# Two slots' score tiles in one visit to the 64-row mode, every second slot, and the places of the probs x values bursts

## The reference

```python
# block L0, 16 heads of 16
q = layer_norm(x, ln1) @ q_w + q_b;  k = ctx @ k_w + k_b;  v = ctx @ v_w + v_b
attn = softmax(where(mask, q @ k.T * 0.25, min))        # 256 x 512 for each head and batch
h = (attn @ v) @ cproj_w + cproj_b + x
h = h + gelu(layer_norm(h, ln2) @ fc_w + fc_b) @ proj_w + proj_b
# block L1, one head of 256, same context
out = h + alpha * (softmax((h @ w_q.T) @ (ctx @ w_k.T).T / 16) @ (ctx @ w_v.T)) @ w_o.T
```

## Time and profile before

| | us |
|---|---|
| median of 3 runs | 340.21 |
| lowest and highest | 338.55, 342.17 |
| the profiled execution | 339.22 |
| its span on the core | 337.4 |
| PE busy | 294.4 (87%) |
| DVE, ACT, POOL busy | 201.4 (60%), 177.4 (53%), 94.0 (28%) |

### The profile page before, as it was taken

How to read it: one execution, slowest core, us unless ns; L and a number is a source line. 1 busy time by engine, 2 the same in 40 slices (tenths; PEclk the granted TensorE clock), 3 DMA queues, 4 the chain that set the end, 5 groups by cost and what they waited for, 6 DMA issues and landing times.

```text
span 337.4 us, 5437 instructions
## 1 busy us (share of the span) xinstructions
PE 294.4 (87%) x2073; PEld 215.1 (64%) x2073; DVE 201.4 (60%) x372; ACT 177.4 (53%) x330; POOL 94.0 (28%) x122
## 2 busy tenths in 40 slices
PE   3996899986977799999968898999989989989895
PEld 2682656753555677656846676665846767768884
DVE  5627856547754867566455787556457464254944
ACT  1431746458453486757351596655545378625612
POOL 2552512103011158430010278420021136143200
PEclk9997559979696999999976999999999699999999
DMA  5799344425502024161130032133030000000001
GB/s 167 193 178 150 92 160 132 106 38 109 143 5 95 25 44 79 30 149 50 28 127 4 26 66 57 59 48 77 14 112 1 3 0 2 2 0 0 2 31 33
DMA packets 14478, 22.26 MB, mean 66 GB/s; under 512 B 3229, under 2 KB 7917, under 8 KB 14429
## 3 DMA queue, kind: packets, MB, share of 16 engines
q1 hardware_dynamic: 10608, 13.97, 19.4%
q0 software_dynamic: 1456, 3.87, 4.2%
q10 hardware_dynamic: 2388, 4.07, 3.8%
HBM read 10.50 MB, written 1.05 MB: 34 GB/s over the span
## 4 chain that ended last, share of the span: by engine, by line
PE 67%; DVE 14%; ACT 6%; issue 5%; POOL 3%; DMA 2%; ACTq 1%; DVEq 0%; POOLq 0%
PE work_ps L620 14%; PE work_ps L607 9%; PE s L676 8%; DVE neg_max L1427 7%; PE om L703 7%; PE work_ps L624 6%; PE s L693 5%; PE s L607 3%; PE s L620 2%; PE om L683 2%; ACT q_stack L1106 2%; PE work_ps L753 1%; POOL max_cols L1746 1%; DVE cT_l L1403 1%; DMA probs<-in_L_xattn_q_w_dram 1%
## 5 line engine op out<-in xcount | busy, mean ns | idle before, releaser
L1427 DVE TENSOR_REDUCE neg_max<-s 128x1 f32<-128x512 f32 x128 | 84.1, 685 | 77.7 <-PE s L676 77.5
L1114 ACT ACTIVATE probs<-s 128x512 f32<-128x512 f32 x128 | 75.1, 597 | 47.0 <-PE s L693 46.3
L693 PE MATMUL s<-q_stack,k_stack 57*128 57x256 f32 x256 | 63.1, 350 | 1.8 <-ACT probs L1114 1.2
L676 PE MATMUL s<-k_stack,q_stack 57*128 57x512 f32 x128 | 59.0, 523 | 3.0 <-DVE neg_max L1427 1.8
L693 PEld LDWEIGHTS s<-q_stack,k_stack 57*128 57x128 f32 x256 | 40.0, 206 | 11.6 <-issue 4.2
L676 PEld LDWEIGHTS s<-k_stack,q_stack 57*128 57x128 f32 x128 | 24.3, 214 | 23.7 <-DVE neg_max L1427 12.8
L703 PE MATMUL om<-probs,vals 128*17 128x256 f32 x512 | 36.0, 403 | 0.1
L1746 POOL CAST max_cols<-neg_max 128x8 fp32r<-128x8 f32 x16 | 5.7, 358 | 96.8 <-DVE neg_max L1427 96.8
L703 PEld LDWEIGHTS om<-probs,vals 128*17 128x17 f32 x512 | 12.2, 100 | 15.6 <-issue 5.7
L1106 ACT ACTIVATE q_stack<-om 8x1024 fp32r<-8x1024 f32 x16 | 16.1, 1008 | 10.2 <-PE om L683 10.1
L1128 ACT ACTIVATE y_h<-work_ps 128x512 fp32r<-128x512 f32 x12 | 7.2, 596 | 15.8 <-PE work_ps L624 14.8
(11 more groups left out here) (317 smaller groups left out, 698.7 us busy)
## 6 DMA issues: line engine op xcount, KB each, us to landing
k_stack<-kp_h SPq DMA_DIRECT2D x32, 128.0 KB
cx<-in_ctx_dram SPq DMA_DIRECT2D x4, 512.0 KB, 4.7
k_stack<-kp_l SPq DMA_DIRECT2D x16, 128.0 KB
q_stack<-qp_h SPq DMA_DIRECT2D x28, 64.0 KB
pcx<-in_ctx_dram ACTq DMA_DIRECT2D x3, 512.0 KB, 4.8
xz<-in_x_dram SPq DMA_DIRECT2D x4, 256.0 KB, 4.1
raw_late<-in_L_xattn_fc_w_dram POOLq DMA_DIRECT2D x1, 1024.0 KB, 5.3
raw_late<-in_L_xattn_proj_w_dram POOLq DMA_DIRECT2D x1, 1024.0 KB, 7.0
```

The source lines that it names most:

```text
L676: pe.matmul(s1[:, s1_bank(b, SLOTS * g + s), :], q_stack[half, hd, chunk(t)], k_stack[half, hd, :], start=True, stop=True).then_inc(s1_ful ...
L693: mm = pe.matmul(s2[:, s2_bank(b, SLOTS * g + s), i * LQ:(i + 1) * LQ], k_stack[half, hd, chunk(k)], q_stack[half, hd, :], start=True, sto ...
L1114: act.activation(probs[:, g % 2, s // 2, k:k + 2, :], s2[:, s2_bank(b, SLOTS * g + s), :].rearrange("p (k n) -> p k n", k=2), ACT.Exp).the ...
L1427: dve.tensor_reduce(neg_max[:, g % 2, s % 2, s // 2:s // 2 + 1], s1[:, s1_bank(b, SLOTS * g + s), :], AX.X, ALU.max, negate=True).then_inc ...
```

## The change

`attend` on PE issues score tiles in slots with even s only, for the slots s and s + 1 together. `MAX_TILES` is now keyed by the even slots, and DVE has a table of its own, `TAKE_AT`, for the slot in which each maximum is taken. Bursts 0 and 1 move from behind the visit of s = 1 to ahead of the visit of s = 0; bursts 2 and 3 from behind the visit of s = 3 to behind the visit of s = 2. The turning of the maxima stays at s = 6 and now comes behind the exp tiles of both 6 and 7. The tables of the pre and post steps and the lists of ACT, POOL and SP are unchanged.

```diff
-MAX_TILES = ((0, 1), (2, 3), (4,), (5,), (6,), (7,), (), ())
+MAX_TILES = {0: (0, 1), 2: (2, 3, 4), 4: (5, 6, 7), 6: ()}
+TAKE_AT = ((0, 1), (), (2, 3), (4,), (5, 6), (7,), (), ())
-PV_AT = {1: (0, 1), 3: (2, 3)}
+PV_BEFORE, PV_AFTER = {0: (0, 1)}, {2: (2, 3)}
@@ PE, attend @@
-                tiles = MAX_TILES[s] if nb < B else ()
-                for i in tiles[:1]:
-                    max_tile(nb, ng, i)
-                if s == 0:
-                    pe.wait_ge(rows_in, NG * b + g + 1)
-                exp_tile(b, g, s)
-                for i in tiles[1:]:
-                    max_tile(nb, ng, i)
-                if s in PV_AT and pb_ >= 0:
-                    for k in PV_AT[s]:
+                if s in PV_BEFORE and pb_ >= 0:
+                    for k in PV_BEFORE[s]:
+                        pv(pb_, pg, k)
+                if s % 2 == 0:
+                    tiles = MAX_TILES[s] if nb < B else ()
+                    for e in range(2):
+                        for i in tiles[e:e + 1]:
+                            max_tile(nb, ng, i)
+                        if s == e == 0:
+                            pe.wait_ge(rows_in, NG * b + g + 1)
+                        exp_tile(b, g, s + e)
+                    for i in tiles[2:]:
+                        max_tile(nb, ng, i)
+                if s in PV_AFTER and pb_ >= 0:
+                    for k in PV_AFTER[s]:
                         pv(pb_, pg, k)
@@ DVE, attend @@
-                    for i in MAX_TILES[s]:
+                    for i in TAKE_AT[s]:
                         take_max(nb, ng, i)
```

## The result

The changed kernel takes 365.95 us in the median of 4 runs (361.64 to 367.77); the kernel before took 339.91 beside it (338.55 to 342.17). The ratio is 1.068, with a 95% interval of 1.055 to 1.080. Slower was forecast, 347 with a range of 332 to 356: the sign was right, and the loss is three times the forecast. Ratios here compare undisturbed runs alone, so a ratio can differ from that of the medians beside it, and the profile of the changed kernel is of its slowest run (367.77), whose span is 28.6 longer than that before where the ratio says 23.

What follows compares the result with a forecast made beforehand. PE's list was taken to bound the kernel. Each middle batch: -3.0 + 8.3 - 1.9 = +3.4, two +6.8; two banks +1.2, batches 0 and 3 nothing; 339.2 + 8.0 = 347 us, range 332 to 356.

Steps and rivals of the forecast that it cites:

- Term 1: PE's list: 62 fewer changes of kind, 0.20 us saved for each; -3.0 in a middle batch, 12.4 at most overall.
- Terms 2 and 3: Each middle batch: new PE waits behind steps, +8.3 us together, and old waits overtaken, -1.9.
- (a): Slot 16: bursts 0 and 1, right behind `F1`, wait for ACT's exponential of s = 7; 1.5 us.
- (b): Slot 18: in the visit behind `F2`, the exp tile of s = 3 waits for the exponential of s = 1; 2.1 us.
- (c): Slot 28, behind `HT`: the exp tile of s = 5 waits for the exponential of s = 3; 0.9 us.
- (d): `S0`, now directly behind `G`, waits for ACT's copy of it; 0.85 us.
- (e): `PT0` waits for ACT's exponential of the second block, which stands behind that of s = 0; 1.2 us.
- term 4: Tiles made for batch 3 need a bank again within a visit, so PE waits for a take; +1.2 us.
- DVE's takes at the head of a group: Bursts ahead of max tiles start DVE's maxima later; priced at a batch's head as 0, bounds -1 to +2 us.
- Term 5: Batches 0 and 3: fewer changes against new waits; taken as 0, bounds -4.8 to +3.4 us.
- Rival 2: Much slower: PE's clock falls to half behind the waits in slots 16 and 18, +10 us, 357; chance 0.14.
- Rivals 1 and 3: First: faster, new waits mostly absorbed, 333 us, chance 0.20. Second: gain and waits nearly balance, 340 to 342, chance 0.16.

Runs made afterwards that it cites:

- ACT's pairs: Merged visits, bursts where they were before, and ACT does both exponentials of a visit at the end of the even slot: 342.08 us, ratio 1.010 to the kernel before.
- the 13 us of DVE's order: Kernel before with only bursts 0 and 1 ahead of the visit of s = 0 (363.71 us), then DVE's takes 0 and 1 moved to s = 1: 350.22, ratio 1.031.
- all at 3: Visits and takes as in the kernel before, all four bursts behind the visit of s = 3: 358.00 us, ratio 1.035.
- the mixed version: Kernel before with visits merged except in batch 0, batch 2's last group and slots 18-21, 28-29 of batches 1 and 2; old burst places: 343.29 us, ratio 1.003.

## Why the prediction was right in sign and wrong in size

- **Term 1** was sized right where it can be seen: a visit of two slots takes 0.66. But it is worth less than it says: the middle batches lost only 2.0 of PE's busy time, where it had 6.0, and all visits merged with old bursts gave 1.003. In the trace of that run batch 1 is 2.3 shorter than before, at PEclk 0.98, and batches 0 and 2 are each over 2 longer, at 0.74 and 0.91. What takes the gain is not shown: with ACT's pairs the waits for ACT inside the visits (0.76 behind `F2`, less elsewhere) were gone, and nothing was gained, though the pairs bring waits of their own. By the rule of the Trainium skill that the prediction named ("TensorEngine Tiling (Array Packing)", Key Properties), taken alone, the time would have fallen to 326.8; no version with fewer changes had a median below that of the kernel before beside it.
- **Terms 2 and 3**, the waits of a middle batch, held one by one: (a) 1.42 for 1.5, (b) 1.28 for 2.1, (c) 0.52 for 0.9, (d) 0.69 for 0.85, (e) 1.26 for 1.2, (f) 0.78 for 0.75, (g) 0.37 and 0.19 for 0.7 at slots 24 and 32, nothing at slot 20, and 0.90 at slot 22 instead. With term 4, the idle time of the two middle batches should have grown by 14.0 and grew by 12.3; they should have lost 8.0 and lost 10.3, because term 1 gave 2.0 for 6.0. But what removes the kernel's loss is not what I had named. Taking away ACT's order behind (a), (b) and (c) left 366; taking the bursts from ahead of the max tiles brought it to 342.
- **DVE's takes at the head of a group**, put at nothing, are one of the two steps that failed. "Bursts 0 and 1 now go ahead of the first max tiles, so DVE starts its two maxima (1.29) later": I priced this once in a batch, in slots 7 to 12, and let it cancel. There that was right: from `OT` to `ZT` batch 1 takes 15.6 with the change and took 15.9, batch 2 15.9 and 17.1. But the same order stands at the head of 14 groups in all, with 1 us of bursts and changes and the wait ahead of them, and DVE's unrelated steps (`kp_l`, `z`, `cT_l`) stand behind the take. Of DVE's other takes I wrote "These cost nothing, unless DVE becomes late for `PJ`", because DVE is busy 60%. That share did not show that its list is blocked at one instruction: PE's wait for `z` went from 0.46 to 2.49. In all, PE's idle time ended by DVE rose in batch 0 (4.7 to 7.5) and batch 3 (2.0 to 4.4); in the two middle batches it did not (11.7 to 11.0), and the waits for ACT came instead.
- **Term 5, batch 0**, is the other: put at one wait of 0.8 at most, measured +14.4. 4.4 of these are idle time, with waits of 2.49 for DVE and of 1.45 to 1.58 for ACT and POOL, and 10.0 are busy time at the lower clock, for which the sum had no term. PE waited for DVE, POOL and ACT in this batch before the change already (11.5 us in all), which may be why each delay lengthens it; no run shows that. Batch 3 and the end together lost 3.1, where the term had +2.6 for batch 3. Its own numbers add up to between +1 and +2, and I took 0 without a reason.
- **Rival 2, the clock**, was right as a mechanism and wrong in its place. I put it behind waits (a) and (b), and there PEclk stayed at 1.00 (from 134.8 to 191.6 in the changed kernel). It fell in batch 0: right behind the wait of 2.49, and from 93.9 on, where waits of 1.51 and 1.58 lie 2 us apart. In the row that I went by, the 0.50 begins at 100.7, ahead of the wait of 1.60 (from 102.5 to 104.1); it lies behind one of 1.76 that ends at 98.91. The Trainium skill ("TensorE: Matmul & The Clock Gate", HAM oscillation — how this bites in real kernels) says that gaps between bursts of matmuls bring the half clock back; the fall to 0.50 behind the wait of 2.49 agrees, and behind the waits of 1.42 and 1.28 there was none.
- **Rivals 1 and 3** are out for the change as a whole. What rival 3 said, that gain and waits balance, is true of the merged visits alone (1.003).

Not settled: how much of the 13 us of DVE's order the kernel before would gain as well, why the clock falls in batch 0 and not behind (a) and (b), and why four bursts together lose with all at 3, where they hold up no max tile that they had not held up before.

## What to carry to other kernels

When work is moved ahead of an instruction in one engine's list, ask what stands behind that instruction's consumer in the consumer's list: one microsecond ahead of a max tile held up DVE's unrelated steps, and through them PE again, wherever PE needed one of them next. A mechanism found at one place of a loop is to be priced at every place where the code repeats it. And the stage in which the first engine waited for three others already (batch 0 here) lost most, two thirds of it in busy time at the lower clock and not in the waits themselves.

## What was not expected of the chip

The same list of a batch took 77.6, 76.4 and 75.2 us at a mean PEclk of 0.93, 0.96 and 0.98. Behind one wait of 2.49 us, eight matmuls took 3.59 us at a PEclk of 0.50, where they had taken 1.97 at 1.00. Matmuls added to batch 0 went with a PEclk of 0.76 there for 0.65, though PE's idle time stayed nearly the same, and cost more than they returned (94.5 against 87.9 us). And fewer changes of kind did not shorten a batch where the clock fell: in the mixed version a batch with 11 changes less (48 against 59) and waits of the same length in sum took 74.1 us, where it took 72.9 before.
